# Two attention layers with routing: two looped stages against one written-out program

## The chip, the cores and the metric

The kernel runs on one core of a Trainium2 chip. The metric is the device time of one execution in microseconds; where several runs are shown their median counts. The core has four engines that compute, TensorE (PE, with PEld for its weight loads), VectorE (DVE), ScalarE (ACT) and GpSimd (POOL), and SyncE (SP), which issues transfers. Each takes its instructions in order, and they wait for one another by semaphores.

## What is computed

The input is x of 32 sequences of 256 tokens and 128 channels, all in fp32. Cut to what matters:

```python
xn = layernorm(x)
s  = two layers of:                      # "layer 0/1" of L0_attn, on xn
       xl = ln(x) * g1 + b1
       q, k, v = xl @ wq + bq, xl @ wk + bk, xl @ wv + bv     # 2 heads of 64
       q, k = rotary(q), rotary(k)       # a factor per channel and position
       x = x + softmax(q k^T / 8) v @ wo
       hid = (ln(x) * g2 + b2) @ w1 + b1h
       x = x + (hid * sigmoid(1.702 hid)) @ w2
logits = xn @ router                     # 64 experts, the 8 best of each token
routed = for each expert: its first 64 tokens through silu(gate) * up @ down, weighted
shared = silu(xn @ wsg) * (xn @ wsu) @ wsd
x  = x + s * silu(routed + shared)
# a second block follows: linear attention, one of 32 experts for each token
```

## The kernel before

The 64 tiles of 128 tokens form 16 pairs (`HALF = 16`); pair i holds two sequences, units g = 0 and 1, of two tiles each (`TPU`). Four stages follow one another.

Stage 1 (`stage1`) runs layer 1 of the attention over the 16 pairs. Its step i does the attention of pair i beside the feed-forward part of pair i - 1. Step 0 and step 15 are written out, steps 1 to 14 are a loop (`bodies`, `Fori`), and a last half step does the feed-forward part of pair 15. The class `x` in each engine's program adds to a step: reading pair i + 1 and its norm (`front`), its router logits, the 8 best of each token (`first`, on VectorE), their exponentials and weights, and the shared expert of pair i. `front` makes two norms of each row, z0 (the norm alone, for router, shared expert and residual) and z1 (its norm once more, for the attention); TensorE turns both, and ScalarE applies gain and shift of the attention's norm to the second. z0 goes by DMA to X, where the residual is held, and to `xw` in DRAM.

Stage 2 (`stage2`) runs layer 2 over the same pairs with the same `body_tensor`, `body_scalar` and `body_vector`. Beside it, its step computes four routed experts: GpSimd gathers their rows (`gather`, an indirect DMA), TensorE goes through gate, up and down, and GpSimd adds the results to `ffn0` (`scatter`). For this the list of each expert's tokens must be there. VectorE makes it between the two layers: `pick_words` ahead of the last half step of stage 1 (it packs 16 tokens in a word and finds an expert's 64 first words by eight rounds of MAX8 and MATCH_REPLACE8 over 512 words), and `pick_tokens` behind the first norms of stage 2 (twice eight rounds over 256 values, with integer shifts between, `split`). Then TensorE turns the list, and VectorE writes `gidx` and `sidx`.

Stages 3 and 4 do the second block. The change doesn't touch their work.

What sets the order is the order of the calls in `body_*`: TensorE does queries and keys of unit 0 (L262) and its values (L266), then turns the second norm of the previous pair (L232), multiplies the feed-forward part (L242, L255) in turn with scores (L277), turns the probabilities (L286), multiplies them with the values (L295) and projects (L304). VectorE multiplies queries and keys by the rotary factors (L415) and adds the bias to the values (L417), takes the maxima of the scores (L424), copies the turned probabilities (L432), adds the residual (L450). ScalarE does the exponentials (L377) and the feed-forward's Silu (L365). In stage 1 L734 and L746 are the shared expert, L782 the logits, L772 the word sums, L852 and L858 to L861 the 8 best and their marks, L401 and L405 the moments of the next rows, L799 the router's exponentials, L873 the shared expert's product. On GpSimd L686 to L701 are `front`, L510 to L516 the second norm (`norm2`).

## Time and profile before

| | |
|---|---|
| runs | 1343.13, 1345.54, 1346.18 us; median 1345.54 |
| profiled execution | 1342.1 us; span of its instructions 1340.3 us |
| granted TensorE clock, mean | 0.96 |
| PE busy | 1165.3 us, 87% of the span |
| DVE busy | 978.6 us, 73% |
| ACT busy | 818.2 us, 61% |
| POOL busy | 652.2 us, 49% |

### The profile page before, as it was taken

How to read it: one execution, taken by the hardware profiler on the slowest of the kernel's cores; microseconds unless marked ns; L12 is line 12 of the kernel's file. 1: busy time of each engine (PE TensorE's matmuls, PEld its weight loads, DVE VectorE, ACT ScalarE, POOL GpSimd, SP SyncE). 2: the span in 40 equal slices, each digit the busy share in tenths (PEclk: the TensorE clock that was granted, in tenths of full speed). 3: DMA queues.
4: the chain of work that ended last, by engine and by line, in shares of the span. 5: the costliest groups of instructions: out<-in, count | busy, mean ns of one | idle time of the engine just before them, and what ended most of it. 6: DMA issues, size and time to landing. Idle time of an engine off the chain costs nothing. (4 is left out here: it accounts for less than half of the span.)

```text
span 1340.3 us, 28601 instructions
## 1 busy us (share of the span) xinstructions
PE 1165.3 (87%) x8326; PEld 933.4 (70%) x8326; DVE 978.6 (73%) x3556; ACT 818.2 (61%) x1993; POOL 652.2 (49%) x1096
## 2 busy tenths in 40 slices
PE   4999999999981799999999984988889889689993
PEld 3777778777771577777777763666667667489993
DVE  3777777777777777777777763788888888657773
ACT  2575665756651365656565652678777787557772
POOL 3443444434321254555454543265665664527775
PEclk9999999999996899999999996999999999889997
DMA  4424233242421122222222212333433433257762
GB/s 163 151 91 152 95 132 119 95 151 88 148 73 34 36 41 63 43 62 44 62 43 63 43 30 68 95 128 120 143 115 130 150 110 131 86 162 232 235 215 67
DMA packets 140732, 141.02 MB, mean 105 GB/s; under 512 B 18662, under 2 KB 119885, under 8 KB 140672
## 3 DMA queue, kind: packets, MB, share of 16 engines
q1 hardware_dynamic: 125248, 111.38, 26.1%
q0 software_dynamic: 14848, 26.77, 7.2%
q10 hardware_dynamic: 576, 2.15, 0.4%
q8 instruction: 28, 0.46, 0.1%
q14 instruction: 32, 0.26, 0.1%
HBM read 67.63 MB, written 62.13 MB: 97 GB/s over the span
## 5 line engine op out<-in xcount | busy, mean ns | idle before, releaser
L377 ACT ACTIVATE pr<-ps,nmx 128x256 f32<-128x256 f32 x256 | 117.9, 473 | 44.3 <-DVE nmx L424 43.7
L365 ACT ACTIVATE big<-ps,BHS 128x256 f32<-128x256 f32 x256 | 107.2, 470 | 60.2 <-PE ps L242 59.5
L242 PE MATMUL ps<-big,W 128*128 128x256 f32 x512 | 129.7, 398 | 5.6 <-ACT big L370 5.5
L255 PE MATMUL ps<-W,big 128*128 128x128 f32 x1024 | 130.6, 281 | 0.0
L255 PEld LDWEIGHTS ps<-W,big 128*128 128x128 f32 x1024 | 119.3, 192 | 13.8 <-ACT big L365 9.9
L2192 POOL DMA_INDIRECT out<-X,io x96 | 102.6, 1068 | 29.6 <-issue 29.6
L242 PEld LDWEIGHTS ps<-big,W 128*128 128x128 f32 x512 | 95.1, 196 | 26.6 <-ACT big L370 15.6
L424 DVE TENSOR_REDUCE nmx<-ps 128x2 f32<-128x512 f32 x128 | 82.4, 686 | 37.6 <-PE ps L277 37.1
L1003 POOL DMA_INDIRECT ffn<-big,si x64 | 93.8, 1466 | 26.4 <-issue 26.4
L432 DVE COPY pT<-ps 128x512 f32<-128x512 f32 x128 | 82.6, 686 | 9.2 <-PE ps L286 8.7
L510 POOL TENSOR_TENSOR big<-big,EPS 128x2 f32<-128x2 f32 x32 | 6.7, 210 | 154.1 <-DVE big L459 154.1
L277 PE MATMUL ps<-qk 64*128 64x256 f32 x512 | 72.6, 402 | 3.0 <-DVE v L417 3.0
L295 PE MATMUL ps<-pT,v 128*64 128x256 f32 x512 | 69.4, 392 | 3.9 <-DVE pT L432 1.1
L262 PE MATMUL ps<-zT,W 128*128 128x256 f32 x256 | 71.7, 404 | 0.0
L286 PE MATMUL ps<-CST,pr 128*128 128x128 f32 x512 | 68.7, 277 | 1.3 <-ACT pr L377 1.3
L370 ACT ACTIVATE big<-ps,COL 128x256 f32<-128x256 f32 x64 | 36.1, 564 | 53.7 <-PE ps L232 53.7
L286 PEld LDWEIGHTS ps<-CST,pr 128*128 128x128 f32 x512 | 56.5, 141 | 16.7 <-ACT pr L377 7.5
L2106 ACT ACTIVATE pr<-ps 128x256 f32<-128x256 f32 x96 | 36.9, 384 | 48.5 <-PE ps L2033 47.4
L450 DVE SCALAR_TENSOR_TENSOR big<-ps,rsm,X 128x128 f32<-128x128 f32 x128 | 39.0, 346 | 34.1 <-PE ps L304 25.2
L415 DVE SCALAR_TENSOR_TENSOR qk<-ps,COL,ROT 128x256 f32<-128x256 f32 x128 | 55.0, 471 | 11.9 <-PE ps L266 9.8
L441 DVE COPY attT<-ps 128x256 f32<-128x256 f32 x64 | 27.2, 425 | 45.3 <-PE ps L295 43.4
L2048 PE MATMUL ps<-big,pr 128*128 x384 | 58.5, 275 | 0.1
(287 smaller groups left out, 3319.1 us busy)
## 6 DMA issues: line engine op xcount, KB each, us to landing
srt<-big SPq DMA_DIRECT2D x16, 1584.0 KB, 5.7
X<-srt SPq DMA_DIRECT2D x24, 800.0 KB
big<-we SPq DMA_DIRECT2D x16, 768.0 KB, 7.3
big<-we SPq DMA_DIRECT2D x16, 384.0 KB, 3.4
X<-srt SPq DMA_DIRECT2D x24, 256.0 KB
big<-x SPq DMA_DIRECT2D x32, 128.0 KB, 2.2
X<-big SPq DMA_DIRECT2D x32, 128.0 KB, 2.1
xw<-big SPq DMA_DIRECT2D x32, 128.0 KB, 1.9
```

The lines of the kernel that those rows point to most:

```text
L242: last = pe.matmul(pb[2 * g + f // 2][:, f % 2 * S:(f % 2 + 1) * S], W0[:, l, 512 + f * P:512 + (f + 1) * P], zT2[:, g, :], start=True, st ...
L255: last = pe.matmul(pb[4 + g][:, t * C:(t + 1) * C], hT[:, g, f, t * P:(t + 1) * P], W0[:, l, 1024 + f * C:1024 + (f + 1) * C], start=(f == ...
L262: pe.matmul(pb[4 + g][:, j * S:(j + 1) * S], w, zT1[:, g, :], start=True, stop=True)
L277: last = pe.matmul(pb[2 * g + h][:, t * S:(t + 1) * S], qk[d, g, 0, t * P:(t + 1) * P], qk[d, g, 1, :], start=True, stop=True)
L286: last = pe.transpose(pb[2 * g + h][:, k * S + t * P:k * S + (t + 1) * P], pr[:, g, h, t, k * P:(k + 1) * P], ident)
L295: last = pe.matmul(pb[2 * g][d, 0:S], v[:, g, k, d], pT[:, g, h, k, :], start=(k == 0), stop=(k == TPU - 1))
L365: act.activation(hT[:, g, f, :], pb[2 * g + half][:, f % 2 * S:(f % 2 + 1) * S], ACT.Silu, bias=BHS[:, l, f:f + 1], scale=GELU).then_inc(s ...
L377: last = act.activation(pr[:, g, h, t, :], pb[2 * g + h][:, t * S:(t + 1) * S], ACT.Exp, bias=nmx[:, g, h * TPU + t:h * TPU + t + 1], accu ...
L424: last = dve.tensor_reduce(nmx[:, g, h * TPU:(h + 1) * TPU], pb[2 * g + h].rearrange("p (t k) -> p t k", t=TPU), X_AXIS, ALU.max, negate=True)
L432: dve.tensor_copy(pT[:, g, h, :, :].rearrange("p k q -> p (k q)"), pb[2 * g + h])\
L1003: pool.indirect_dma_start(out=ffn0[:, :], out_offset=bass.IndirectOffsetOnAxis(ap=si[:, n:n + 1], axis=0), in_=ye[half, n // 2, :], in_off ...
L2192: pool.indirect_dma_start(out=out[:, :], out_offset=bass.IndirectOffsetOnAxis(ap=io[b][:, k:k + 1], axis=0), in_=ob[b][:, k, :], in_offset ...
```

## The change

Both layers become one block in which no engine has a loop. Step n = 0 to 31 (`FR = 32`) does the attention of pair n (layer 1) or n - 16 (layer 2) beside the feed-forward part of step n - 1; a step 32 ends it. In particular:

- `fronts(n)` says which pairs are read and normed in step n: one before step 0, two in each of steps 0 to 6, one in step 7, none in 8 to 14, and from step 15 on one of layer 2. `routed(n)` are the pairs whose 8 best are found in step n, those of `fronts(n - 1)`. So routing is done after step 8. Turned rows wait in `ring`, which holds ten pairs.
- Only z1 is turned. The router's and shared expert's weights have their mean over the channels taken off, and a factor `root` per token gives them back what the second norm took: it scales the router's exponentials and the shared expert's two halves, which are now computed with tokens on partitions (192 columns) and turned afterwards (`shared_turn`). The gain g1 is multiplied into wq, wk and wv, and b1 with the three biases comes in through one row added to those weights (`shifts` on PE, `fold` on DVE): the queries and keys are only multiplied by the rotary factors, and the values are only copied, now by ScalarE.
- z0 is written by GpSimd straight into X; the copies of X and of xin by DMA fall away, and layer 2's moments are read from X.
- The search is cut in 20 pieces (`search(n, k)`), four in each of steps 9 to 13 (`PICK` = 9, `KEYS` = 14). The later rounds look at `work[:, 8 * r:]` or `work[:, 8 * r:32 * (r + 1)]`, no longer at the whole. The list is turned at the end of step 14.
- The token weights are multiplied by GpSimd (`token_weights`), and the sums over an expert's marks become one product and one reduction.
- `stage3` and `stage4` only find the bias row at another place.

The diff, cut to its core:

```diff
-        def bodies(engine, step, between=None):
-            step(0, ffn=False)
-            with engine.Fori(1, HALF - 1) as i:
-                step(i)
-            step(HALF - 1, front=False)
-            if between:
-                between()
-            step(HALF, att=False)
...
+        FR = HALF + HALF
+        FRONT_ROOM = 4
+        RING = 10
+
+        def fronts(n):
+            if n < 0:
+                return [0]
+            if n < HALF - 1:
+                return [p for p in (2 * n + 1, 2 * n + 2) if p < HALF]
+            return [n + 1] if n + 1 < FR else []
+
+        def routed(n):
+            return [p for p in fronts(n - 1) if p < HALF]
+
+        R_STEPS = HALF // 2 + 1
...
+                    def front(n, k, p):                                   # GpSimd
+                        pool.wait_ge(s["stats1"], p + 1)
...
+                        for t in range(2 * TPU):
+                            last = pool.tensor_scalar(z1[k][:, t, :], xin[:, p % FRONT_ROOM, t, :], nm1[:, k, t:t + 1],
+                                                      rs1[:, k, 1, t:t + 1], ALU.add, ALU.mult)
+                        last.then_inc(s["z1"], 1)
+                        for t in range(2 * TPU):
+                            last = pool.tensor_scalar(x_tile(p, t // TPU, t % TPU), xin[:, p % FRONT_ROOM, t, :],
+                                                      nm1[:, k, t:t + 1], rs1[:, k, 0, t:t + 1], ALU.add, ALU.mult)
+                        last.then_inc(s["xn"], 1)
...
+                    for n in range(HALF):
+                        if 0 < n <= R_STEPS:
+                            token_weights(n - 1)
+                        for k, f in enumerate(fronts(n)):
...
+                        for g in range(2):
+                            norm2(n, g)
...
+                        if att:                                           # TensorE, a step
+                            pe.wait_ge(s["xl1"], n + 1)
+                            if 0 < n <= HALF:
+                                pe.wait_ge(s["ff"], n)
+                            queries(0)
...
+                            values(0)
...
+                        if n == PICK + 1:
+                            pe.wait_ge(s["folded"], 3)
...
+                        if ffn:
+                            turn2(0)
...
+                            prob_turn(0)
+                            if early_layer:
+                                pe.wait_ge(s["v_sb"], u + 2)
+                                shared_hidden(n, 1)
...
+                            attention(0)
+                            prob_turn(1)
+                            project(0)
+                        if ffn:
+                            hidden_out(1)
+                        if att:
+                            if early_layer:
+                                shared_turn(n)
...
+                            attention(1)
+                            for k, f in enumerate(fronts(n)):
+                                if k:
+                                    pe.wait_ge(s["hsT"], n + 1)
+                                turn1(f, k)
...
+                                shared_down(n)
...
+                            project(1)
+                            for k, f in enumerate(fronts(n)):
+                                if f < HALF:
+                                    logits(f, k)
+                            if n < R_STEPS:
+                                token_words(n)
...
+                            values(1)                                     # ScalarE, a step
+                            probs(0)
+                            if n < R_STEPS:
+                                token_exps(n)
...
+                            probs(1)
+                            if early_layer:
+                                shared_gates(n)
+                                shared_turned(n)
...
+                    def best(n):                                          # VectorE
...
+                        for m in range(k):
+                            for t in range(2 * TPU):
+                                dve.max(out=mx8[:, m, t, :], in_=lg[:, m, t, :])
...
+                    def chosen(n):
+                        k = len(routed(n))
+                        for m in range(k):
+                            for t in range(2 * TPU):
+                                dve.match_replace(out=rep[:, m, t, :], in_to_replace=mx8[:, m, t, :],
+                                                  in_values=lg[:, m, t, :], imm_value=NEG)
+                        dve.drain()
+                        dve.tensor_scalar(kk[:, 0:k, :, :], rep[:, 0:k, :, :], NEG / 2, None, ALU.is_lt).then_inc(s["key"], 1)
...
+                    def search(n, k):
+                        at = 4 * (n - PICK) + k
+                        if at == 0:
+                            word_values()
+                        elif 1 <= at <= 8:
+                            first_words(at - 1, at)
+                        elif at == 9:
+                            split(4, 3.0, 16, True)
+                        elif 10 <= at <= 13:
+                            first_parts(2 * (at - 10), 2 * (at - 10) + 2)
+                        elif at == 14:
+                            split(1, 4.0, 1, False)
+                        elif 15 <= at <= 18:
+                            first_parts(2 * (at - 15), 2 * (at - 15) + 2)
...
+                        if att:                                           # VectorE, a step
+                            heads_of(0)
+                            if n < R_STEPS:
+                                best(n)
...
+                            if PICK <= n < KEYS:
+                                search(n, 0)
+                            heads_of(1)
+                            if fronts(n):
+                                dve.wait_ge(s["z1"], fronts_through(n - 1))
+                                stats(n, rows_of)
+                            if n < R_STEPS:
+                                chosen(n)
+                            if PICK <= n < KEYS:
+                                search(n, 1)
+                            largest(0)
+                        if ffn:
+                            result(0)
+                        if att:
+                            largest(1)
+                            turned(0)
+                            sums(0)
+                            attended(0)
+                            if PICK <= n < KEYS:
+                                search(n, 2)
+                            turned(1)
+                            sums(1)
+                            if early_layer:
+                                shared_products(n)
...
+                            residual(0)
+                            attended(1)
+                            moments(0)
+                        if ffn:
+                            result(1)
+                        if att:
+                            residual(1)
...
+                            moments(1)
+                            if n < R_STEPS:
+                                weighed(n)
+                            if PICK <= n < KEYS:
+                                search(n, 3)
```

## Rows read from the trace of the kernel before

**Rows 1.** Stretches: length, busy PE, PEld, DVE, ACT, POOL (instructions), PEclk, DMA.

```profile
205.64:229.41 23.77, 23.48 (x172) 18.77 (x169) 17.85 (x72) 15.00 (x42) 9.80 (x22) 1.00 0.35 118
397.00:441.28 44.28, 11.07 (x59) 8.60 (x59) 34.36 (x107) 6.12 (x12) 6.94 (x12) 0.62 0.10 29
```

**Rows 2.** Timeline of PE, first product of steps (start, length, engine, line, names, shapes).

```profile
18.29 2.02 PE L262 MATMUL ps<-zT,W 128*128 128x256 f32 x4
...
39.27 1.13 PE L262 MATMUL ps<-zT,W 128*128 128x256 f32 x4
...
205.64 1.13 PE L262 MATMUL ps<-zT,W 128*128 128x256 f32 x4
...
460.02 1.13 PE L262 MATMUL ps<-zT,W 128*128 128x256 f32 x4
...
779.10 1.13 PE L262 MATMUL ps<-zT,W 128*128 128x256 f32 x4
```

**Rows 3.** Timeline of PE around and in the step that starts at 205.64.

```profile
201.82 0.66 PE L232 MATMUL ps<-CST,big 128*128 128x128 f32 x4
...
202.75 1.06 PE L746 MATMUL ps<-WSD,big 96*128 96x128 f32 x8
...
204.39 1.10 PE L782 MATMUL ps<-WS,big 128*128 128x64 f32 x8
...
205.42 0.29 PE L772 MATMUL ps<-SUM,kk 128*64 128x8 bf16 x4
...
216.99 1.10 PE L734 MATMUL ps<-big,WS 128*96 128x256 f32 x4
...
217.93 1.04 PE L286 MATMUL ps<-CST,pr 128*128 128x128 f32 x8
```

**Rows 4.** Timeline of DVE and ACT in the same step.

```profile
209.72 0.59 DVE L852 MAX8 big<-big 128x8 f32<-128x64 f32 x4
...
211.62 0.87 DVE L401 BATCH_NORM_STATS2 big<-big 128x6 f32<-128x128 f32 x4
...
212.85 0.84 DVE L415 SCALAR_TENSOR_TENSOR qk<-ps,COL,ROT 128x256 f32<-128x256 f32 x2
...
214.06 1.29 DVE L424 TENSOR_REDUCE nmx<-ps 128x2 f32<-128x512 f32 x2
...
215.38 0.47 ACT L377 ACTIVATE pr<-ps,nmx 128x256 f32<-128x256 f32 x1 [0.26 <-DVE nmx L424]
...
217.20 1.07 ACT L799 ACTIVATE big<-big 128x64 f32<-128x64 f32 x4
...
222.91 0.72 DVE L873 TENSOR_TENSOR big<-ps,big 96x256 f32<-96x256 f32 x2
```

**Rows 5.** Timeline of POOL: second norm, and the next pair's front.

```profile
204.60 0.88 POOL L516 TENSOR_SCALAR att<-big 128x128 f32<-128x128 f32 x2 [0.17 <-issue]
...
213.02 0.20 POOL L686 TENSOR_TENSOR big<-big,EPS 128x4 f32<-128x4 f32 x1 [3.61 <-DVE big L405]
...
218.40 0.88 POOL L701 TENSOR_SCALAR z<-big 128x128 f32<-128x128 f32 x2
```

**Rows 6.** The search on DVE: first, last row, and its two costliest groups.

```profile
397.35 0.68 DVE L602 SCALAR_TENSOR_TENSOR big<-big,CST 64x512 f32<-64x512 f32 x1
...
442.98 0.17 DVE L1196 COPY gi<-gidx 128x2 int32<-128x2 int32 x1
...
L564 DVE MAX8 big<-big 64x8 f32<-64x256 f32 (+1 forms) x24 | 12.2, 508 | 1.8
L567 DVE MATCH_REPLACE8 big<-big 64x256 f32<-64x256 f32 (+1 forms) x21 | 10.3, 490 | 0.0
```

**Rows 7.** Timeline of PE: second tile of gathered rows, layer 2.

```profile
609.50 0.33 PE L1054 MATMUL ps<-CST,big 128*128 128x128 f32 x1 [0.29 <-DMA big<-xw,gi]
```

**Rows 8.** Lengths of two products in stage 3 (shortest, median, longest, ns).

```profile
L1816 DVE TENSOR_TENSOR W<-W x16: 181/914/1299, 859.0 to 1157.6; 128x32 f32<-128x32 f32 x16
...
L1371 POOL TENSOR_TENSOR big<-big,X x14: 1267/1279/1288, 840.1 to 1099.5; 128x512 f32<-128x512 f32 x14
```

More of the change, by code:

```diff
@@ new lines, in _ @@
+                    pe.wait_ge(ld_first, 32)
+                    turn1(0, 0)
+                    pe.wait_ge(ld_fold, 48)
+                    pe.wait_ge(s["consts"], 1)
+                    pe.matmul(pb[1][:, 0:E0 + 2 * F0], mean_of[:, :], WS[:, :], start=True, stop=True)
+                    shifts(0, 0)
+                    pe.wait_ge(s["folded"], 1)
+                    logits(0, 0)
+                    pe.wait_ge(s["folded"], 2)
+                    for n in range(FR + 1):
+                        step(n)
@@ new lines, in token_exps @@
+                    def token_exps(n):
+                        act.wait_ge(s["lmax"], n + 1)
+                        if n:
+                            act.wait_ge(s["wrow"], n)
+                        for k, p in enumerate(routed(n)):
+                            for t in range(2 * TPU):
+                                last = act.activation(ex[:, k, t, :], lg[:, k, t, :], ACT.Exp, bias=nl[:, k, t:t + 1],
+                                                      scale=root[:, p, t:t + 1])
+                        last.then_inc(s["lexp"], 1)
@@ new lines, in _ @@
+                    act.dma_start(CST[:, 0:C_BLK], cst[:, 0:C_BLK]).then_inc(ld_first, 16)
+                    act.dma_start(W0[:, 0, :], w0[:, 0:1536]).then_inc(ld_fold, 16)
+                    act.dma_start(CST[:, C_BLK:], cst[:, C_BLK:]).then_inc(ld_w, 16)
+                    act.dma_start(W0[:, 1, :], w0[:, 1536:3072]).then_inc(ld_late, 16)
+                    act.wait_ge(s["consts"], 1)
+                    front(0, 0)
+                    logits(-1)
+                    for n in range(FR + 1):
+                        step(n)
@@ new lines, in _ @@
+                    stats(-1, rows_of)
+                    dve.wait_ge(s["consts"], 1)
+                    dve.wait_ge(ld_first, 32)
+                    shifted(0)
+                    dve.wait_ge(s["fold"], 1)
+                    dve.tensor_tensor(WS[:, :], WS[:, :], pb[1][:, 0:E0 + 2 * F0], ALU.add).then_inc(s["folded"], 1)
+                    fold(0, 0)
+                    for l in range(DEPTH):
+                        dve.tensor_scalar(BHS[:, l, :], COL[:, l * NCOL + BH:l * NCOL + BH + FC], GELU, None, ALU.mult)
@@ L2221, in pack @@
     for l in range(DEPTH):
[L2222 removed]
+        c += [a[f"L0_attn_{n}"][l][:, None] for n in ("ln1_g", "ln1_b", "ln2_g", "ln2_b")]
         c.append(a["L0_attn_b1"][l].reshape(FC, P).T)
```

1522 lines of the change are left out of this document (701 added, 821 removed).

## Prediction

> **What bounds the kernel now.** I read the busy time by stretch first. A step of layer 1 lasts 23.77 us and TensorE is busy for 23.48 of them, VectorE for 17.85, ScalarE for 15.00, GpSimd for 9.80; between the layers lies a stretch of 44 us in which TensorE is busy for a quarter and its clock is granted at 0.62 of full speed, while VectorE is busy for 34 us [rows 1]. Then the starts of the steps on TensorE: step 0 at 18.29, step 1 at 39.27, step 8 at 205.64 (166.37 / 7 = 23.77 each); layer 2's step 1 at 460.02 and its step 15 at 779.10 (319.08 / 14 = 22.79 each) [rows 2]. Behind layer 2 the diff touches only the place of some bias columns, so stages 3 and 4 (some 520 us) stay. What counts is when step 1 of layer 2 starts, and the length of the steps behind it.
>
> **The seam.** Step 0 and fifteen steps of 23.77 end at 18.29 + 20.98 + 356.55 = 395.8. If layer 2's first step followed at its own 22.8 us, step 1 would start at 418.6; it starts at 460.0. The seam costs 41.4 us. It is the search: VectorE goes through it from 397.35 to 442.98 [rows 6], and TensorE has nothing else to do. The new program runs step 16 right behind step 15, so all 41.4 us go. The rest of this part is what the step lengths give back.
>
> **TensorE's work per step.** A transposition costs 0.93 / 8 = 0.116 us (201.82 to 202.75, front), the four logits products 1.03, the word sums 0.22, one pair's half of the shared hidden products 0.94 (216.99 to 217.93) [rows 3]. Removed: four of the eight front transpositions (one norm is turned, not two). The shared hidden products become 192 columns wide from 256, so I scale 0.94 to 0.70, twice a step. Added: four transpositions of the shared product (0.47). A step that brings in no pair loses 0.93 + 1.03 + 0.22 and the net 0.01 of the shared part: 23.77 - 2.2 = 21.6. I add 0.4 for two waits: the values' copy, now on ScalarE ahead of the second norm's, and the copy of the turned probabilities, 1.98 us behind the start of their transpositions (217.93), which the shorter shared product covers less. That makes 22.0. Each pair brought in adds 0.47 + 1.03 + 0.22 = 1.7, so a step with two pairs holds 25.4 us of TensorE.
>
> **Steps 1 to 6, two pairs each.** Here VectorE's order decides. Time T counts from the step's first product (205.64). Now VectorE does best, chosen, marks (209.72 to 211.62, 1.90 for four tiles) and the moments of the rows (to 212.85, 1.23) before the second unit's queries and keys, at T 7.2; the first softmax maximum starts at T 8.42, just when the scores are there [rows 4]. In the new order the second unit's queries and keys come at T 5.5, when its values are multiplied, and end at 6.35; but behind them, ahead of the maximum, stand the moments of eight tiles (2.5) and eight replacements with the marks (2.3). The maximum starts at T 11.2, 2.8 us later. It takes 1.3, and the first head's exponentials another 1.04, so TensorE's transpositions, due at T 12.2, begin at 13.6 and end at 15.05 instead of 13.1. Next ScalarE puts the router's exponentials between the two units: 1.07 for four tiles [rows 4], 2.13 for eight. The second unit's exponentials so run from 16.65 to 18.6 (1.82 for four, 215.38 to 217.20, and the last read-out), and its transpositions end at 19.15 instead of 16.25. 2.9 us are lost; nothing behind catches them up, since TensorE's queue is in order. 25.4 + 2.9 = 28.3, with 0.1 at the loose ends 28.4.
> GpSimd in these steps: one pair's front now takes 213.02 to 219.28, 6.3 us [rows 5], the new one about 7.4 with the four small products for the folded scale. Two from T 8.4 end at 23.2, before the moments of the second norm at 24.6; nobody waits.
> Step 0 (one pair routed, two fronts, no feed-forward) goes by the same chain from 21.0 to 24.7; step 7 (two routed, one front) to 25.5.
>
> **Steps 8 to 15.** With no front behind it, TensorE comes sooner to turning the second norm than this is ready: from the end of the second unit's attention (201.82) to the normed rows (204.60 + 0.88 = 205.48) pass 3.66 us [rows 3, 5], and TensorE has 3.04 left of work (0.99 + 0.64 + 0.97 + 0.44). 22.0 + 0.7 = 22.7. Step 8 has one pair's words: 22.9.
> Steps 9 to 13 carry the search. MAX8 and MATCH_REPLACE8 of the old one are busy 12.2 and 10.3 us [rows 6]; with splits and drains it is 35 us. The last two thirds now look at 32 to 200 elements, not 256, which I estimate at half: 29 us, in 20 pieces of about 1.5. Of a step's four pieces the first is covered by the wait for the values, the second ends at T 8.4, before the scores, the fourth by the wait of the next step. The third stands before the copy of the second unit's probabilities and so before the shared products. Those are ready at T 18.0 now (222.91 + 0.72) [rows 4], but TensorE now wants them turned ahead of the second attention, at T 18.9; with 1.5 more they come at 19.9. That costs 1.05: 23.75 a step. The fold of layer 2's weights (products in step 9, a wait at the head of step 10) and the split in step 12 add 2.1 together. Sum 120.8. Steps 14 and 15: 22.9 and 23.2 (the list's turning, and the first front of layer 2).
>
> **Sum to layer 2.** 24.7 + 6 x 28.4 + 25.5 + 22.9 + 120.8 + 22.9 + 23.2 = 410.4, against 377.5. So 32.9 of the 41.4 us go back. The start: fewer transpositions, but two small products and the fold of layer 1's weights ahead of the first queries, at half clock: 0.3 later (bounds -1 and +3). Net 8.2 gained.
>
> **Layer 2's steps.** The products are the same. The values' copy on ScalarE frees TensorE from a wait for VectorE, but TensorE then meets the gathered rows, for which it waits already [rows 7]. Between 0 and 0.5 a step; I take 0.25, 4.0 for sixteen. The loops themselves show no cost that TensorE feels: the first products of the looped step at 205.64 and of the written-out one at 779.10 both take 1.13 [rows 2].
> Total 12.2. The profiled execution took 1342.1 us (span 1340.3), the median of the runs is 1345.5, 3.4 more: 1342.1 - 12.2 = 1329.9 in its terms, 1345.5 - 12.2 = **1333.3** in the median's.
>
> **A lock.** In stage 3 VectorE's L1816, 128x32, takes 0.18 us at best and 1.30 at worst, as long as GpSimd's 128x512 product of 1.27 beside which it runs [rows 8]. The new step gives GpSimd such a product (the token weights). It falls at about T 3 to 4.3, where VectorE waits anyway, so I cost it at 0; if it hit the chain, 1.1 in each of nine steps is 10 us, which the range holds.
> The Trainium skill ("SBUF — State Buffer", Who interferes with whom) says why: a VectorE instruction with two SBUF inputs and a GpSimd one that reads SBUF exclude each other for the whole instruction. By that rule the trace agrees, and the change, which doubles GpSimd's reading in steps 1 to 6, would sooner lose than gain.
> The skill also speaks for the change ("Runtime: NRT & Kernel Launch", Instruction fetch mechanics): taken branches can stall the fetch, so full unrolling is preferred. By rows 2 the layers' loops lose nothing on TensorE, so I give it nothing.
>
> **Rivals.** (1) TensorE stays the bound in the two-pair steps, because VectorE and ScalarE come earlier than I order them: 25.4 in steps 1 to 6 (-18.0), 22.5 in step 0 and 23.9 in step 7 (-3.8), the search covered altogether (-5.6), and 0.5 a step in layer 2 (-4.0). 1333.3 - 31.4 = 1302. For it: TensorE is busy 99% of a step now, VectorE 75% [rows 1]. Against it: 4.8 us of VectorE's work ahead of the maximum, with 2.8 us of reach.
> (2) Slower: the search isn't covered. Its place is steps 9 to 13, where VectorE would have 14.3 + 5.8 of 23.8 us to do, in order, with four crossings to TensorE. If every piece lengthens its step, 29 us fall on the path instead of 5.6: 1333.3 + 23.4 = 1357. It decides from 18 us (5.6 + 12.2). Against it: now VectorE is idle a quarter of each step, and routing is gone from these. Half of it, with the lock, gives the time of before.
> That the search isn't moved after all can't be: its first piece waits only for words that are complete after step 8.
>
> **How the numbers follow.** My sum, 1318 to 1342.8: 0.47. Rival 1, below that: 0.27. No change, within 0.2% (1342.8 to 1348.2, about what can be told here): 0.12. Slower, rival 2 whole or in part: 0.14. Faster is 0.47 + 0.27 = 0.74. The range leaves out a tenth on either side: 1302 to 1353. The sum's own range is 1318 to 1343.
>
> **What would show it.** Layer 2's step 1 starts at 452 of the span, with no stretch of low clock before it. TensorE's steps 1 to 6 are 28 us apart, with its waits at the transpositions of probabilities for ScalarE's exponentials, and steps 9 to 13 about 24, with a wait for the shared product. Layer 2's steps are 22.5. Wrong would be: steps 1 to 6 at 25 or 26 (rival 1), any step of 9 to 13 over 27 (rival 2), GpSimd's front later than the second norm's moments, or waits without a releaser that a fetch of instructions would leave.

## The result and the profile after

The changed kernel takes 1330.9 us (median; 1327.4 to 1332.4), the kernel before in the same session 1345.0: a ratio of 0.9895, 95% interval 0.9882 to 0.9908. The prediction was 1333.3. In the profiled executions the time fell from 1342.1 to 1327.4 us, the span from 1340.3 to 1325.6; the prediction's term for that is 12.2, measured are 14.7. Two of its larger terms were off, in opposite directions, so that the total is nearer than the sum deserves.

Starts of steps on TensorE in the changed kernel (they answer to [rows 2]; the columns are start, length, engine, line, names, shapes):

```profile
17.95 1.08 PE L567 MATMUL ps<-big,W 128*128 128x256 f32 x4
...
96.85 1.13 PE L567 MATMUL ps<-big,W 128*128 128x256 f32 x4
...
231.56 1.13 PE L567 MATMUL ps<-big,W 128*128 128x256 f32 x4
...
442.66 1.13 PE L567 MATMUL ps<-big,W 128*128 128x256 f32 x4
...
766.27 1.13 PE L567 MATMUL ps<-big,W 128*128 128x256 f32 x4
```

These are steps 0, 3, 8, 17 (layer 2's step 1) and 31. Layer 2's step 1 starts at 442.66 instead of 460.02: 17.4 us are won by there. Its step 15 starts at 766.27 instead of 779.10: 12.8. So layer 2 gives 4.5 us back; the stages behind it give 1.8 us more.

Stretches of the changed kernel (they answer to [rows 1]; length, busy time of PE, PEld, DVE, ACT and POOL with instructions, PEclk, DMA share, GB/s): a two-pair step, step 8, a step with the search, the place of the old seam, and layer 2's fourteen steps from 1 to 14.

```profile
96.85:124.27 27.42, 25.32 (x188) 20.21 (x185) 20.08 (x86) 18.05 (x49) 17.97 (x41) 1.00 0.41 133
231.56:253.86 22.30, 21.71 (x159) 17.50 (x156) 15.85 (x53) 15.09 (x42) 3.98 (x10) 1.00 0.28 93
326.37:350.67 24.30, 21.95 (x152) 17.25 (x153) 18.26 (x65) 13.68 (x36) 3.95 (x11) 1.00 0.22 79
400.00:445.00 45.00, 42.91 (x311) 33.39 (x310) 30.09 (x101) 28.64 (x75) 10.80 (x21) 1.00 0.14 46
442.66:766.27 323.61, 302.25 (x2186) 228.57 (x2185) 220.41 (x742) 204.79 (x532) 165.48 (x224) 1.00 0.20 41
```

The seam is gone: at 400 to 445 us TensorE is busy for 42.9 of 45 us at full clock. The two-pair step has TensorE busy for 25.3 us (25.4 were summed), and lasts 27.4. What it waits for in that step, and in layer 2's steps 1 to 14 (us in total, times, longest):

```profile
PE ps L617 <- ACT pr L839: 1.7, 4, 0.9
PE ps L627 <- DVE pT L1095: 0.2, 1, 0.2
```

```profile
PE ps L572 <- ACT big L811: 7.4, 6, 1.7
PE ps L627 <- DVE pT L1095: 4.6, 14, 0.6
PE ps L510 <- DMA big<-xw,gi: 3.3, 9, 0.9
```

L617 turns the probabilities and waits for the exponentials: the wait that was forecast. L572 multiplies the values of the next step and waits for L811, the experts' outputs on ScalarE, for 1.2 us on the mean in six of the steps: a wait that was not forecast. The kernel before waits there too (L266 for L1137), but never for more than 0.2 us.

### The profile page after: what moved, and what is told of

It reads as the page before. It is cut to its first block and busy times, and to the rows that moved or that the text cites. A ratio compares the mean times of both kernels' runs of the same rounds, so it can differ in the third digit from the quotient of the medians.

```text
span 1325.6 us, 26420 instructions
## 1 busy us (share of the span) xinstructions
PE 1162.5 (88%) x8336; PEld 934.7 (71%) x8336; DVE 939.0 (71%) x3368; ACT 838.4 (63%) x2011; POOL 669.3 (50%) x1153
## 5 line engine op out<-in xcount | busy, mean ns | idle before, releaser
L586 PE MATMUL ps<-big,W 128*128 128x256 f32 x512 | 130.4, 399 | 7.8 <-ACT big L832 7.8
L839 ACT ACTIVATE pr<-ps,nmx 128x256 f32<-128x256 f32 x256 | 117.6, 472 | 27.4 <-DVE nmx L1087 26.6
L420 POOL DMA_INDIRECT ffn<-big,si x64 | 93.4, 1459 | 23.4 <-issue 23.4
L617 PE MATMUL ps<-CST,pr 128*128 128x128 f32 x512 | 72.5, 281 | 14.6 <-ACT pr L839 14.6
L617 PEld LDWEIGHTS ps<-CST,pr 128*128 128x128 f32 x512 | 56.9, 143 | 33.2 <-ACT pr L839 27.7
L1080 DVE TENSOR_TENSOR qk<-ps,ROT 128x256 f32<-128x256 f32 x128 | 48.0, 416 | 35.6 <-PE ps L572 35.3
L567 PE MATMUL ps<-big,W 128*128 128x256 f32 x256 | 68.8, 391 | 0.7
L627 PEld LDWEIGHTS ps<-pT,v 128*64 128x64 f32 x512 | 34.0, 137 | 33.3 <-issue 26.0
L608 PEld LDWEIGHTS ps<-qk 64*128 64x128 f32 x512 | 44.1, 186 | 17.3 <-issue 10.3
```

Of the source, the lines that this page charges most:

```text
L420: pool.indirect_dma_start(out=ffn0[:, :], out_offset=bass.IndirectOffsetOnAxis(ap=si[:, n:n + 1], axis=0), in_=ye[half, n // 2, :], in_off ...
L567: pe.matmul(pb[4 + g][:, j * S:(j + 1) * S], m, ring[:, n % RING, g * S:(g + 1) * S], start=True, stop=True)
L586: last = pe.matmul(pb[2 * g + f // 2][:, f % 2 * S:(f % 2 + 1) * S], W0[:, lf, 512 + f * P:512 + (f + 1) * P], zT2[:, g, :], start=True, s ...
L608: last = pe.matmul(pb[2 * g + h][:, t * S:(t + 1) * S], qk[d, g, 0, t * P:(t + 1) * P], qk[d, g, 1, :], start=True, stop=True)
L617: last = pe.transpose(pb[2 * g + h][:, k * S + t * P:k * S + (t + 1) * P], pr[:, g, h, t, k * P:(k + 1) * P], ident)
L627: last = pe.matmul(pb[2 * g][d, 0:S], v[:, g, k, d], pT[:, g, h, k, :], start=(k == 0), stop=(k == TPU - 1))
```

## Experiments

Whole times are ratios to the kernel before on the same chip. Step lengths are differences of starts on TensorE. In layer 1 they repeat within 0.03 us from run to run, but for step 0, which took 23.97 to 25.27 us in six runs that leave it as it is. Ratios from different sessions differ by as much as several of the effects (the changed kernel itself gave 0.9895 and 0.9857), so the experiments are read by the steps.

### The level for the comparisons

> The changed kernel unaltered, beside the three others on their chip, as the level that they are held against. 1327 to 1333 us. Its layer-2 steps should again take 23.1 us on the mean, 22.6 and 23.6 to 24.0 in turn, and the third scatter of each step should again land 4 to 6 us after its issue.

Measured: 1367.5 us, where the kernel before takes 1387.9 on that chip: 0.9857 (0.9825 to 0.9889). The layers are the same (two-pair steps 27.42, layer 2's steps 23.11 on the mean). Nearly all of the extra time lies behind them: from the start of step 31 to the end of the span some 594 us, 559 in the first profile. Steps may be compared between these chips, whole times may not.

### Layer 2: who delays the experts' outputs

The gate weights of the next step are a load of 384 KB on SyncE's queue. The kernel before issues it behind the wait for the next pair's normed rows; the written-out program issues it as soon as the last gate product is done. Two kernels tell whether that matters, one for each program. GpSimd adds the four experts' results to `ffn0` by four scatters a step, and each waits for the one before it to land.

```
# e_gates_late: the changed kernel
    sp.wait_ge(s["eg"], i + 1)
+   sp.wait_ge(s["ehTp"], i + 1)
    gates(i + 1)
```

> One wait added on SyncE in layer 2: the next step's gate weights are issued when the experts' hidden rows have been turned, some 5 us later, in place of at the moment when the last gate product is done. Nothing else is changed. Theory (the load collides with a scatter): in the changed kernel that load is issued 0.4 us behind the third scatter of the step, which lands 4 to 6 us later, where the kernel before has 3.0. With the load moved away the scatter should land after 3.0 to 3.3 us, GpSimd's wait ahead of the fourth should shrink from 3.7 to about 1.5 us, ScalarE's wait for the scatters ahead of the experts' outputs should go, and the layer-2 steps should take 22.6 to 22.8 in place of 23.1: 4 to 6 us less in all, about 1326 us. Rival (the written-out layer 2 stalls on fetching its instructions, 35 such packets against 8 in the kernel before): nothing changes in the steps, within 1 us of the unaltered kernel.

```
# b_gates_early: the kernel before
-   if not last:
-       sp.wait_ge(s["z1"], base + 2 * i + 4)
-       rows(i + 2)
    sp.wait_ge(s["eg"], i + 1)
    gates(i + 1)
+   if not last:
+       sp.wait_ge(s["z1"], base + 2 * i + 4)
+       rows(i + 2)
```

> The kernel BEFORE with the two lines of SyncE's layer-2 loop swapped: the gate weights are issued as soon as the last gate product is done, and the load of the rows behind it. The converse of the late gates. Theory (collision): the third scatter of a step lands after 4 to 6 us in place of 3.0 and the layer-2 steps grow by 0.2 to 0.5 us, 3 to 7 us in all, though the layer is a loop with hardly a fetch. Rival (instruction fetches): no difference, 0 plus or minus 1 us.

Measured: late gates 0.9831 (0.9808 to 0.9854; the changed kernel on the same chip 0.9857), early gates in the kernel before 1.0011 (0.9994 to 1.0028). Below are a third and a fourth scatter of GpSimd (L420 of the changed kernel, L421 of the late gates, L1003 of the kernel before with early gates; the small GpSimd instruction between them waits for the third to land). First the changed kernel with SyncE's load:

```profile
594.94 1.51 POOL L420 DMA_INDIRECT ffn<-big,si  x1 [0.18 <-issue]
600.13 0.19 POOL L406 TENSOR_TENSOR carrier<-carrier 128x1 f32<-128x1 f32 x1 [3.69 <-DMA ffn<-big,si]
600.88 1.44 POOL L420 DMA_INDIRECT ffn<-big,si  x1 [0.56 <-issue]
```

```profile
595.35 0.38 SPq L306 DMA_DIRECT2D big<-we  x1
```

The late gates, a step without and a step with an instruction fetch beside the scatter:

```profile
570.15 1.51 POOL L421 DMA_INDIRECT ffn<-big,si  x1 [0.18 <-issue]
573.25 0.19 POOL L407 TENSOR_TENSOR carrier<-carrier 128x1 f32<-128x1 f32 x1 [1.59 <-DMA ffn<-big,si]
574.00 1.43 POOL L421 DMA_INDIRECT ffn<-big,si  x1 [0.56 <-issue]
...
592.62 1.51 POOL L421 DMA_INDIRECT ffn<-big,si  x1 [0.18 <-issue]
596.47 0.26 POOL L407 TENSOR_TENSOR carrier<-carrier 128x1 f32<-128x1 f32 x1 [2.34 <-DMA ffn<-big,si]
597.22 1.54 POOL L421 DMA_INDIRECT ffn<-big,si  x1 [0.49 <-issue]
```

The kernel before with early gates:

```profile
590.38 1.51 POOL L1003 DMA_INDIRECT ffn<-big,si  x1 [0.18 <-issue]
594.56 0.23 POOL L983 TENSOR_TENSOR carrier<-carrier 128x1 f32<-128x1 f32 x1 [2.67 <-DMA ffn<-big,si]
595.31 1.43 POOL L1003 DMA_INDIRECT ffn<-big,si  x1 [0.52 <-issue]
```

From the third scatter's issue to the fourth's pass 3.85 us with the load elsewhere (574.00 - 570.15), 4.93 with it in the kernel before (595.31 - 590.38), 5.94 in this step of the changed kernel. The kernel before shows it even unaltered, in step 14 of layer 2, where its last load of gate weights has no wait for rows ahead of it: the load comes 0.39 us behind the third scatter, and the fourth is issued 4.8 us after it, with no packet of instructions near.

```profile
771.28 0.39 SPq L945 DMA_DIRECT2D big<-we  x1
```

That the load delays the scatter, by 1.1 us, is thus shown in both directions. In the changed kernel its removal shortens layer 2's steps from 23.12 to 22.81 us, 4.2 us over steps 1 to 14, as expected, and TensorE's wait for the experts' outputs falls from 7.4 us to:

```profile
PE ps L573 <- ACT big L812: 1.6, 2, 1.3
```

But the converse missed: in the kernel before the same 1.1 us lengthen the layer's steps by 0.5 us in all, from 319.1 to 319.6 for steps 1 to 14, not by 3 to 7. All of it is in one step, step 2, which takes 23.61 us in place of 22.77; the other thirteen together take 0.3 us less. So a scatter 1.1 us late is absorbed by itself. What is special about step 2 is the step ahead of it: there a packet of instructions came 2.7 us behind the third scatter, and the fourth was issued 6.5 us after the third. (The Trainium skill, "DMA: Bandwidth & Descriptors", SWDGE vs HWDGE vs iDMA, says that each DMA engine takes its queues in turn, GpSimd's and SyncE's among them; that a scatter has to share with a load fits it, but no run looked inside a DMA engine.)

Such packets are the changed kernel's second delay. Instructions are fetched by DMA. In layer 2's steps 1 to 14 the written-out program has 18 packets of 16 KB, one every 18 us, and 13 of 8 KB; the loop has 1 and 2. On the mean 256 instructions of TensorE lie between two of the large ones, so they are taken for its own (the Trainium skill, "Runtime: NRT & Kernel Launch", Instruction fetch mechanics, gives blocks of 16 KiB for 256 instructions: the trace agrees).

In the changed kernel's profile three of the third scatters take 5.1 to 5.8 us to land (at 502.6, 594.9 and 711.3) and two of the fourth 4.2 and 4.7 (484.6, 669.7), where others take 3.8 to 4.2 and 2.9 to 3.3. Each of the five has a large packet 1.5 to 3.6 us behind its issue; with one 1.2 us behind, a fourth scatter took 3.2 and 3.3 us, and with one 3.9 us behind a third took 4.1. Each of the five is in the step before one of 23.6 to 24.0 us; the steps without are 22.6 to 22.8, but for one of 23.4 that follows a long one. From the issue of the third scatter to the landing of the fourth pass 9.0 to 9.7 us ahead of the long steps and 7.5 to 8.2 ahead of the others, though all have the load beside them. So here too the load alone costs nothing, and it is the load and a packet together that reach TensorE. The two experiments on fetches:

```
# e_more_fetches: on the late gates, on SyncE
    downs(i + 1)
+   for _ in range(200):
+       sp.wait_ge(s["ey"], i + 1)
```

> The kernel with the late gate loads (its layer-2 steps took 22.81 us on the mean), and on SyncE, which has nothing to do there, 200 waits more in each layer-2 step that are met already, so that more instructions must be fetched while layer 2 runs; nothing else. Theory (16 KB instruction packets that fall into a scatter delay it, and this is what is left of layer 2's slower steps: in the late-gates run the gap from the third to the fourth scatter was 3.8 us in most steps and 4.5 to 4.9 in the three with a fetch 1.7 us behind the third scatter): some 12 KB more a step, more such gaps, and steps of 22.9 to 23.2 us, 2 to 5 us more than without. Rival (a fetch costs the scatters nothing): 22.8 us again.

Measured: 0.9871 (0.9853 to 0.9889); 88 KB more were fetched (half of what was expected), and layer 2's steps took 22.86 us: no more than 0.7 us for all fourteen. That is the rival's number, but it doesn't speak for the rival. The added packets are of 8 KB, none of 16, and none came within 4 us behind a third or fourth scatter, so the kernel doesn't test what a large packet beside a scatter does. The gaps of 4.5 to 4.9 us stood again in the 3rd, 7th and 12th step, each with a 16 KB packet 1.7 to 1.9 us behind the third scatter, and the 4th, 8th and 13th step were long (24.25, 23.92, 23.02). So it isn't the amount fetched that counts.

```
# e_best_shifted: on the combined version below, on TensorE
+   if n == 14:
+       for _ in range(64):
+           pe.wait_ge(s["consts"], 1)
```

> The combined version and 64 waits on TensorE, met already, at the head of step 14 and nothing else: they cost a few us there, and every later 16 KB instruction packet of TensorE comes 64 instructions, about a fifth of a step, earlier against the work. In the combined version two of layer 2's steps 1 to 14 are long, the 4th (23.04 us) and the 8th (23.49), the others 22.61; each follows a step, the 3rd and the 7th, whose third scatter had such a packet 1.9 us behind it and whose fourth scatter came 4.8 us after the third in place of 3.8. Theory (the packet delays the scatter): with the packets elsewhere the gaps in the 3rd and 7th step go back to 3.8 us and the 4th and 8th step to 22.6; other steps may get long, but only behind a step with a packet 1.5 to 2 us after its third scatter. Rival (the data of these experts, or the memory, makes them long): the 4th and 8th step stay at 23.0 and 23.5 us.

Measured: 0.9788 (0.9765 to 0.9811). The edit did not do what it was for. Most packets moved against the work, by 0.9 to 5.6 us, but not the two in question: they still came 1.7 us behind the third scatters of the 3rd and 7th step, and these had gaps of 4.99 and 4.57 us again, with a long step behind the 3rd (23.52) and 22.77 and 22.90 behind the 7th. That tells nothing apart. One packet did come nearer to a scatter, in the 11th step, from 2.6 to 1.5 us behind it; its gap rose from 3.92 to 4.48 us and the 12th step from 22.61 to 23.05 us.

One case for the theory, no case against it. The rival of the last expectation, the experts' data, is answered by the loop: it works on the same data, and its steps are all 22.7 to 22.9 us. Three levels can be set side by side. Fourteen steps of 22.61 us would be 316.5 us. The fetches with the load out of the way take 319.4 (the late gates), the fetches with the load 323.6, and the load almost without fetches adds 0.5 to the loop. That the load delays the scatter is shown, and that its removal gives 4.2 us. That the fetches are the other half is argued: it goes with the long steps, but no run took the fetches out of the written-out program.

### Two-pair steps: which order sets them

```
# e_chosen_late, steps 0 to 8 on VectorE
-   chosen(n)
    search(n, 1)
    largest(0)
    result(0)
+   chosen(n)
    largest(1)
```

> The changed kernel with one move on VectorE, in steps 0 to 8: the replacements and marks of the chosen experts (1.9 to 2.3 us for two pairs) stand behind the first softmax maximum and the first unit's result and ahead of the second maximum, in place of ahead of the first. Theory (the prediction's: in two-pair steps VectorE's routing ahead of the maximum sets TensorE's first turning of probabilities, and all behind it): the first maximum starts at about T 8.4 in place of 10.2, the exponentials come 1.7 us earlier, and the two-pair steps take 25.7 to 26.0 us in place of 27.4; with step 0, 7 and 8 that is 9 to 13 us less, about 1320 us. Rival 1 (GpSimd's two fronts, which end 22.2 us into the step, or ScalarE's chain to the shared gates catch it up): under 0.7 us a step, 4 us in all. Rival 2 (the marks come too late for the second maximum and cost there what they save here): no change.

Measured: 0.9834 (0.9808 to 0.986). Two-pair steps take 26.49 us in place of 27.42, short of the 25.7 to 26.0 of the theory. The first maximum starts at T 8.5 (101.95 in the step from 93.47), as the theory had it; but the marks now stand ahead of the second maximum and the first copies of turned probabilities, and the wait moved there, as rival 2 says in part:

```profile
PE ps L627 <- DVE pT L1095: 1.7, 1, 1.7
```

```
# e_chosen_after_products, steps 0 to 8 on VectorE
-   chosen(n)          # ahead of largest(0)
    shared_products(n)
+   chosen(n)
```

> The changed kernel with the replacements and marks of the chosen experts still later on VectorE, in steps 0 to 8: behind the shared products and ahead of the first unit's residual. In the run with the late marks the two-pair steps fell from 27.42 to 26.49 us only; TensorE then waited 1.7 us for VectorE's copies of the turned probabilities, which the marks (2.1 us) had pushed back. Theory (VectorE's order is the bound of these steps, and the marks have no hurry): that wait goes too, and the two-pair steps take 25.4 to 25.8 us, 11 to 14 us less than the changed kernel over steps 0 to 8. Rival (ScalarE's router exponentials, 2.7 us ahead of the shared gates, now set the shared product, wherever the marks stand): 26.2 to 26.5 us, no better than the late marks.

Measured: 0.9823 (0.9806 to 0.984). Two-pair steps take 26.13 us. Steps 0 to 16 take 9.2 us less (415.5 against 424.7); 2.2 of that are step 0, which differs by up to 1.3 us between runs of the same order. TensorE's waits in the step:

```profile
PE ps L627 <- DVE pT L1095: 0.4, 1, 0.4
PE ps L636 <- DVE attT L1104: 0.3, 1, 0.3
PE ps L617 <- ACT pr L839: 0.3, 1, 0.3
```

The wait of 1.7 us became one of 0.4; a new one, 0.3 for the second unit's attended values, is the price of the marks' new place. The result lies between the two numbers on record, nearer to the rival's; the residual waits are on three engines, and no single one is the bound any more.

```
# e_exps_last, steps 0 to 8 on ScalarE
-   token_exps(n)
    probs(1)
+   token_exps(n)
```

> The changed kernel with the router's exponentials behind the second unit's softmax exponentials on ScalarE, in steps 0 to 8, in place of between the two units. Theory 1 (the prediction's term: they delay the second unit's exponentials and so TensorE's second turning, where it waits 0.9 us): the two-pair steps take 26.4 to 26.6 us in place of 27.42. Theory 2 (they stand ahead of the shared gates in either order, and these set the shared product that TensorE turns next): that wait goes, but TensorE waits for the shared product instead, and the steps take 27.1 to 27.3 us.

Measured: 0.9862 (0.9845 to 0.9879). Two-pair steps take 27.26 us: theory 2. TensorE reaches the second turning earlier, and then waits for the shared product:

```profile
PE ps L549 <- DVE big L958: 1.1, 1, 1.1
PE ps L617 <- ACT pr L839: 0.5, 2, 0.3
```

A wait of 0.9 us for the exponentials was worth 0.15 us, since 2.8 us of other exponentials stand ahead of the shared gates either way.

### The search

```
# e_third_moved, steps 9 to 13 on VectorE
+   search(n, 2)
    attended(0)
-   search(n, 2)
    turned(1)
```

> The changed kernel with the search's third piece of each step ahead of the copy of the first unit's attended values, where VectorE waits 1.2 us, in place of behind it and ahead of the second copies of probabilities. Theory (the prediction's term for steps 9 to 13: the third piece delays those copies and so the shared product; 0.5 to 0.7 us of wait in the trace, 1.05 predicted): steps 9, 10 and 12 get 0.4 to 0.7 us shorter, 1.5 to 3 us in all. Rival (the piece is hidden anyway and the steps are long for another reason, the fold and the first piece): under 0.5 us in all.

Measured: 0.9861 (0.9833 to 0.989). Steps 9 to 13 take 116.5 us together in place of 120.0: 0.79, 0.74, 0.44, 0.95 and 0.55 us less. That is the theory, and a little more than it said. In the changed kernel the piece and its victims stand thus (step from 278.61):

```profile
295.98 0.64 DVE L973 MAX8 big<-big 64x8 f32<-64x472 f32 x1
...
296.76 0.63 DVE L976 MATCH_REPLACE8 big<-big 64x472 f32<-64x472 f32 x1
297.46 1.29 DVE L1095 COPY pT<-ps 128x512 f32<-128x512 f32 x2
...
298.75 0.96 DVE L958 SCALAR_TENSOR_TENSOR big<-ps,big 128x96 f32<-128x96 f32 x4
```

```profile
299.77 0.64 PE L549 MATMUL ps<-CST,big 128*96 128x128 f32 x4 [0.53 <-DVE big L958]
```

The piece (1.4 us) stands in front of the copies, these in front of the shared products (L958), and TensorE waits 0.53 us for them.

```
# e_no_search: the changed kernel; the lists are constants
-   word_values(), first_words(), split(), first_parts()
+   lst = 128 r + expert + 1
```

> The changed kernel with the whole search left out: the lists of the experts' tokens are filled with constants (distinct tokens), so the experts work on other rows than the reference's, as many as before. Steps 9 to 13 then cost what a step with neither routing nor search costs. Theory (search covered but for the third piece and the fold): steps 9 to 13 fall from 120.0 us together to 112.5 to 114, that is 6 to 7.5 us for the whole search and fold, of 34 us that it keeps VectorE busy; the fold stays, with 1 to 1.5 of it. Rival (wholly covered, other causes lengthen the steps): under 2 us.

Measured: 0.9834 (0.9818 to 0.9851). Steps 9 to 13 take 114.3 us: the whole search costs 5.7 us in the changed kernel, a little less than expected. 3.5 of them are the third pieces' place. Most of the rest is in step 10, where VectorE does a first piece of the search ahead of the fold of layer 2's weights (L919): TensorE waits 1.6 us for it there, with the third piece moved as well, and not at all without the search.

```
# b_no_search: the kernel before, the same constants
-   pick_words(dve)
-   largest(...); split(...); largest(...)
+   lst = 128 r + expert + 1
```

> The kernel BEFORE with its search left out: the lists are filled with the same constants (distinct tokens) as in the changed kernel without its search, so the experts work on other rows than the reference's, as many as before. It prices the seam. Theory (the prediction's: the search keeps VectorE busy for some 35 us with TensorE idle, and is on the path altogether): layer 2's step 1 starts 33 to 36 us earlier, at 424 to 427 of the span, and the time falls by as much, to about 1311 us; 5 to 8 us of the seam of 41.4 are the end of the one program and the start of the other. Rival (part of the seam is loads and first norms behind the search that come no earlier): less than 28 us.

Measured: 0.983 (0.9807 to 0.9854). Layer 2's step 1 starts at 439.78, only 20.2 us earlier: the rival. The products there on TensorE, and two stretches:

```profile
397.40 3.78 PE L242 MATMUL ps<-big,W 128*128 128x256 f32 x8 [0.65 <-ACT big L370]
...
405.84 3.90 PE L255 MATMUL ps<-W,big 128*128 128x128 f32 x32
417.03 1.52 PE L232 MATMUL ps<-CST,z 128*128 128x128 f32 x4 [7.28 <-DVE z L1168]
```

```profile
396.00:410.00 14.00, 12.35 (x52) 9.84 (x52) 2.19 (x16) 4.38 (x10) 2.01 (x5) 0.64 0.04 11
410.00:419.77 9.77, 1.86 (x9) 0.88 (x9) 4.40 (x17) 1.17 (x3) 4.90 (x9) 0.65 0.34 104
```

Even without a search the seam costs some 21 us. The last pair's feed-forward runs alone for 14 us, at a clock of 0.64: four of its products (x8) take 3.78 us, twice, where the full clock needs some 2.0. Then 9.8 us pass until the first product of layer 2, with a load of rows from DRAM (VectorE waits 3.09 us for it), their moments, GpSimd's power and the normed rows, for which TensorE waits 7.28 us.

The kernel before had a higher clock there:

```profile
396.82 3.55 PE L242 MATMUL ps<-big,W 128*128 128x256 f32 x8 [0.66 <-ACT big L370]
...
401.37 1.99 PE L242 MATMUL ps<-big,W 128*128 128x256 f32 x8 [0.66 <-ACT big L370]
```

Its clock from 396 to 410 is 0.88, and its feed-forward lasts 2.5 us less (11.2 against 13.7). The kernel before with early gates, whose work there is the same, has 0.63 and both times 3.78, and yet layer 2 starts 402.0 us after step 1 in both: beside a search the clock of the feed-forward costs nothing. Without the search it does: 2.5 of the 21 us are a clock that was not the same in two profiles of the same work.

### Together

> Three of the edits together on the changed kernel: the marks behind the shared products, the search's third piece ahead of the copy of the attended values, the gate weights issued late. If each removes a wait of its own, their gains in the steps add: 9 to 10 us in steps 0 to 8 (26.13 in place of 27.42 a two-pair step), 3.5 in steps 9 to 13, 3 to 4.5 in layer 2 (22.8 in place of 23.1 a step): 1312 to 1315 us on a chip where the kernel before takes 1345, a ratio of 0.976 to 0.978. Rival (a later wait swallows part): 1318 us or more.

Measured: 1310.9 us (1308.2 to 1311.9), 0.9766 (0.975 to 0.9782). The gains add: the span is 16.5 us shorter than the changed kernel's, and 9.2, 3.5 and 4.2 make 16.9. Steps as expected (26.12 two pairs, 116.8 for steps 9 to 13 with a step 9 of 24.3), layer 2 from step 1 to 15:

```profile
93.28:119.40 26.12, 24.95 (x187) 20.27 (x184) 20.28 (x84) 18.07 (x49) 18.17 (x42) 1.00 0.44 142
...
431.09:748.95 317.86, 302.72 (x2187) 228.69 (x2185) 220.22 (x742) 205.38 (x533) 165.19 (x224) 1.00 0.20 42
```

317.86 us for fourteen steps are 22.70 each; twelve of them take 22.60 to 22.64.

## Why the prediction was right, and where it was not

- **The seam.** "So all 41.4 us go" held: layer 2's step 16 of the program starts right behind step 15. "It is the search" did not: without it half of the seam stays (some 21 us). [rows 6] show VectorE searching from the seam's start to its end, and I took the engine that was busy for the cause. Its first quarter ran beside a feed-forward that TensorE was doing alone, in part at half clock, and the rest beside a restart that waits for a load. The term came out right although its reason was half wrong, because written-out steps remove all three.
- **The start.** 0.3 later was taken; it is 0.3 earlier (17.95 against 18.29). Between runs it moves by more than that.
- **Step 0 and steps 1 to 6.** Predicted 24.7 and 28.4, measured 24.08 and 27.41. The chain is the forecast one, link by link, 1 us shorter: the second unit's heads at T 5.2, moments of eight tiles 2.4 in place of 2.5, replacements and marks 2.1 in place of 2.3, the first maximum at T 10.2 in place of 11.2, the turning at 12.6 in place of 13.6. Moving the marks takes the wait away: shown.

```profile
102.05 0.76 DVE L1080 TENSOR_TENSOR qk<-ps,ROT 128x256 f32<-128x256 f32 x2 [1.34 <-PE ps L572]
102.72 1.64 DVE L894 BATCH_NORM_STATS2 big<-big 128x6 f32<-128x128 f32 x8
...
106.68 0.43 DVE L941 TENSOR_SCALAR kk<-big 128x512 bf16<-128x512 f32 x1
107.03 1.28 DVE L1087 TENSOR_REDUCE nmx<-ps 128x2 f32<-128x512 f32 x2
```

```profile
109.42 0.66 PE L617 MATMUL ps<-CST,pr 128*128 128x128 f32 x4 [0.24 <-ACT pr L839]
...
113.87 0.66 PE L617 MATMUL ps<-CST,pr 128*128 128x128 f32 x4 [0.93 <-ACT pr L839]
```

  "Nothing behind catches them up, since TensorE's queue is in order" was too strong for the second wait: with the exponentials moved it was worth 0.15 us, not 0.9.
- **GpSimd.** Fronts of 7.1 us in place of 7.4, ended at T 22.2 (23.2 predicted), and GpSimd, at the second norm at 120.77, waits 1.71 us for VectorE: nobody waits for GpSimd, as said.
- **Steps 7, 8, 14, 15.** 25.05, 22.30, 22.68 and 23.93 against 25.5, 22.9, 22.9 and 23.2. The wait for the second norm is 0.3 us at most, not 0.7; step 8 has none. Step 15 waits 1.1 us for the places of the list, which I had at half that.
- **Steps 9 to 13.** 120.0 against 120.8. The mechanism (third piece, copies, shared product) is shown; its price is 3.5 us for five, not 5.25. The fold and the split, taken at 2.1, cost 3.3: with the third piece moved steps 9, 10 and 12 take 1.3, 1.3 and 0.7 us more than the 22.64 of step 11. The search as a whole costs 5.7 of 34 us: rival 2 (29 us on the path) falls. (That rival's "half of it, with the lock, gives the time of before" was added wrongly: half of 23.4 us gives 1345.0 by itself, with the lock 1355.)
- **Sum to layer 2.** 402.5 us for steps 0 to 15 in place of 410.4: of 41.4 us 25.0 go back, not 32.9. The miss is 6.5 us in steps 0 to 6 and small ones behind, all to the same side but for step 15. Rival 1 (25.4 us a step) was wrong for the kernel as written; the run with the marks moved comes within 0.7 us of it.
- **Layer 2's steps.** The term of the wrong sign: 22.5 predicted, 23.12 measured (22.79 before), 8.5 us in all: 4.0 that did not come and 4.5 lost. Undisturbed steps take 22.61 us where the kernel before has 22.71 at its shortest. If that is the values' copy on ScalarE, which no run had alone, it is worth 0.1 us, not 0.25. The failed step is "the products are the same": I costed what moved on the five engines and not what moved on SyncE's queue, where a 384 KB load lost the wait that kept it clear of a scatter; nor did I cost the written-out program's fetches, with which that load collides. The text asked for "waits without a releaser" as the sign of fetches; in the changed kernel they stand beside DMAs that land late.
- **The lock.** Costed at 0, and it is off the path: VectorE's small product (L931) takes 0.40 us beside GpSimd's product of 1.04 (L400), some 0.2 us more than at its shortest (0.16; 0.94 at its longest), ahead of a wait of 1.3.

```profile
100.31 0.40 DVE L931 TENSOR_TENSOR big<-big 128x8 f32<-128x8 f32 x1
```

```profile
99.64 1.04 POOL L400 TENSOR_TENSOR big<-big 128x512 f32<-128x512 f32 x1
```

- **Written-out loops.** The Trainium skill ("Runtime: NRT & Kernel Launch", Instruction fetch mechanics) prefers full unrolling, because taken branches can stall the fetch. I gave that nothing, and the looped steps show no stall. In layer 2 unrolling rather costs: the fetches that it brings stand ahead of the long steps, as told above.

The forecast of 12.2 us was near 14.7 because 9.2 us more than forecast were won by layer 2's step 1, 8.5 fewer in its steps, and 1.8 came from behind it, where nothing was forecast. That the first two cancel is luck; the range of 1302 to 1353 would have covered either alone.

## What to carry to other kernels

An engine that is busy through a gap need not be its cause: take its work out, or ask at each moment of the gap what would run if it were not there. When a loop is written out or a wait is dropped as no longer needed, look at what that wait kept apart: list the moment of every large DMA against the small ones that others wait for, before and after, and the fetches with them. Of a wait that an edit is to remove, name the next one on the same queue: here waits of 0.9 and 1.7 us were worth 0.15 and 0.9, until the marks went where VectorE was idle.

## What the runs showed of the hardware that I had not expected

- A scatter of 64 rows by GpSimd's queue lands 3.0 us after its issue, and 3.8 to 4.2 us after it with a 384 KB load issued 0.4 to 0.7 us behind on SyncE's. With a 16 KB packet of instructions in the same microseconds as well it took 5.1 to 5.8 us; with the packet and without the load (packets 1.5 to 1.9 us behind, in the two combined versions and the one with more fetches) 3.7 to 4.2.
- At the lower level of the granted clock the feed-forward's four products (x8) took 3.78 us against 1.99 at full clock. TensorE had waited 1.8 us before them. The same stretch of the same work had a clock of 0.88 in one profile of the kernel before and of 0.63 in another with only a load moved elsewhere, a difference of 2.5 us in the feed-forward.
- A turning in two halves, of which the second waits 0.26 us for its own exponentials, takes 1.57 us on TensorE from its start to its end (109.42 to 110.99; the ends are modelled) in place of 1.04 in one piece.
- On one chip both kernels took 37 to 43 us longer, with layer 1's steps behind the first equal to 0.03 us; 34 of the changed kernel's 37 us lay in the last two stages.
